# Cutting each head's loads into pieces and moving the projections away from the start of a half, in a Trainium2 attention kernel

## The reference, cut to what matters

```python
heads, dim_head = (16, 64)
x = layer_norm(x, ln_m_g, ln_m_b)          # the context, 6404 rows of 128
lat = layer_norm(latents, ln_l_g, ln_l_b)  # the tokens, 1024 rows of 128
q = lat @ Wq
kv_input = jnp.concatenate([x, lat], axis=1)   # 7428 keys
kv = kv_input @ Wkv
k, v = jnp.split(kv, 2, axis=-1)
dots = jnp.einsum('bhid,bhjd->bhij', q, k) * scale
attn = jax.nn.softmax(dots, axis=-1)
out = jnp.einsum('bhij,bhjd->bhid', attn, v)
return out @ Wout
```

## Time and profile before

| | |
|---|---|
| median of three runs | 2502.02 us |
| the profiled execution | 2494.57 us, span 2492.8 us |
| attention heads (first L608 to last L1000) | from 119.4 us to 2107.9 us |
| TensorE busy | 2303.6 us, 92% of the span |
| VectorE, ScalarE, GpSimd busy | 1864.0, 1673.9, 1846.9 us |
| moved by DMA | 165.57 MB |

### The profile page before, as it was taken

One profiled execution on the slowest core, in us unless ns is written; L12 is line 12 of the kernel. 1 busy time (PEld: TensorE's weight loads), 2 busy tenths in 40 slices (PEclk: granted clock), 3 DMA queues, 4 the chain that ended last, 5 costly groups with the idle time before them and its releaser, 6 DMA issues. The chain is left out here.

```text
span 2492.8 us, 68127 instructions
## 1 busy us (share of the span) xinstructions
PE 2303.6 (92%) x27961; PEld 1491.0 (60%) x27961; DVE 1864.0 (75%) x2822; ACT 1673.9 (67%) x3037; POOL 1846.9 (74%) x1105
## 2 busy tenths in 40 slices
PE   2999999999999999999999999999999998689987
PEld 1365665566566655665666556655666556558875
DVE  8877777887787878877877787878777761467754
ACT  4677777777677777776777677767777776246642
POOL 1798888989888988898889888888889998120000
PEclk9899999999999999999999999999999999889988
DMA  2612223132413141414131413141313000600000
GB/s 87 164 40 57 72 79 99 49 83 67 111 38 96 56 122 36 97 56 122 36 93 60 118 40 94 61 117 40 93 61 88 2 2 10 186 10 2 2 4 9
DMA packets 107639, 165.57 MB, mean 66 GB/s; under 512 B 23544, under 2 KB 97216, under 8 KB 102208
## 3 DMA queue, kind: packets, MB, share of 16 engines
q1 hardware_dynamic: 104032, 157.12, 23.0%
q10 hardware_dynamic: 3296, 4.10, 0.5%
HBM read 99.22 MB, written 61.97 MB: 65 GB/s over the span
## 5 line engine op out<-in xcount | busy, mean ns | idle before, releaser
L608 POOL TENSOR_TENSOR att_prob_low<-att_prob 128x1024 f16<-128x1024 f32 x960 | 1765.5, 1865 | 230.0 <-PE all_banks L728 126.4
L885 ACT ACTIVATE att_prob<-all_banks 128x512 f32<-128x512 f32 x1888 | 1070.7, 591 | 366.3 <-PE all_banks L693 247.7
L979 DVE TENSOR_REDUCE att_part<-all_banks 128x2 f32<-128x1024 f32 x800 | 946.5, 1218 | 197.9 <-PE all_banks L653 197.9
L714 PE MATMUL all_banks<-att_v,att_prob 128*128 128x129 f16 x5664 | 584.1, 221 | 2.8 <-DVE shared_att L1003 0.6
L714 PEld LDWEIGHTS all_banks<-att_v,att_prob 128*128 128x128 bf16 x5664 | 414.6, 98 | 238.0 <-issue 10.8
L728 PEld LDWEIGHTS all_banks<-att_v,att_prob_low 128*128 128x128 f16 x7552 | 328.8, 98 | 138.4 <-POOL att_prob_low L608 18.7
L674 PE MATMUL all_banks<-att_qc,att_kc 128*128 128x512 f16 x1056 | 401.3, 380 | 0.0
L675 PE MATMUL all_banks<-att_qd,att_kd 128*128 128x512 f16 x1056 | 401.0, 380 | 0.0
L728 PE MATMUL all_banks<-att_v,att_prob_low 128*128 128x65 f16 x7552 | 386.0, 194 | 13.4 <-POOL att_prob_low L608 13.4
L718 PE MATMUL all_banks<-att_v,att_prob 128*128 128x64 f16 x1888 | 371.2, 197 | 0.0
L716 PE MATMUL all_banks<-att_v,att_prob 128*128 128x65 f16 x1888 | 365.9, 194 | 0.0
(11 more groups left out here) (304 smaller groups left out, 3074.8 us busy)
## 6 DMA issues: line engine op xcount, KB each, us to landing
att_kc<-k_high SPq DMA_DIRECT2D x30, 928.5 KB, 10.8
att_v<-v_all SPq DMA_DIRECT2D x14, 1870.5 KB
v_all<-att_stage_v SPq DMA_DIRECT2D x98, 258.0 KB, 2.4
att_kd<-k_low SPq DMA_DIRECT2D x16, 928.5 KB, 15.0
k_high<-att_stage_h SPq DMA_DIRECT2D x98, 128.0 KB, 1.7
k_low<-att_stage_l SPq DMA_DIRECT2D x98, 128.0 KB, 1.9
att_kd<-k_low SPq DMA_DIRECT2D x16, 208.0 KB, 15.7
prep_ctx<-in_ctx SPq DMA_DIRECT2D x5, 640.0 KB, 9.1
```

What stands on the lines that cost most here:

```text
L608: pool.tensor_tensor(prob_low[g % NL][:, 0:w], p[:, 0:w], p.bitcast(BF16)[:, 1:2 * w:2], op=ALU.subtract).then_inc(low_split, 1)
L714: pe.matmul(O[:, q, :], w, v[:, e, t, :], start=first, stop=False, skip_group_check=True)
L885: act.activation(prob[g % NP][:, i * BANK:(i + 1) * BANK], S[n % 3], ACT.Exp, scale=SCALE)\
L979: dve.tensor_reduce(parts[:, n:n + 2], pers.banks[:, 4 + 2 * pair:6 + 2 * pair, :], axis=AX.X, op=ALU.max)\
```

## The change

The 7 transfers of `load_kq` become 16 and the 2 of `load_v` become 5: kc (twice) and the low part of K in four quarters each, and V in four parts and its tail. In each of periods 0 to 7 SyncE issues two pieces of K and Q. The pieces of V follow one per period, from period 8 in an even head and from period 24 in an odd one. From period 1 on SyncE first waits until the scores before that period are done, with a projection or without. The lists of periods are new: period 0 has no task in any head, and period 15 has none either. The counts in the waits on `k_in` and `v_in` follow.

```diff
-        KQ_AT = sorted([*range(0, PERIODS, 2), 9, 19])
-        V_AT = [w for w in range(23) if w % 3 != 2 and w != BACK_AT]
+        KQ_AT = [1, 3, 5, 7, 9, 11, 12, 14, 16, 17, 19, 20, 22, 23, 25, 26, 28]
+        V_AT = [1, 3, 4, 6, 7, 9, 10, 12, 14, 16, 17, 19, 20, 22, 23]
+        KQ_PIECES, V_PIECES, FIRST_K = 16, 5, 4
...
-            def load_kq(m):
+            def load_kq(m, x):
                 e = m % 2
-                sp.dma_start(kc[0:DH, e, 0:KEYS], k_high[rows(m), :]).then_inc(k_in[e], 16)
-                sp.dma_start(kc[DH:P, e, 0:KEYS], k_high[rows(m), :]).then_inc(k_in[e], 16)
-                sp.dma_start(qc[0:DH, e, :], q_high[rows(m), :]).then_inc(q_in[e], 16)
-                sp.dma_start(qc[DH:P, e, :], q_low[rows(m), :]).then_inc(q_in[e], 16)
-                sp.dma_start(qd[DH:P, e, :], q_high[rows(m), :]).then_inc(q_in[e], 16)
-                sp.dma_start(kd[DH:P, e, 0:KEYS], k_low[rows(m), :]).then_inc(k_in[e], 16)
-                load_upper(m)
+                c = slice(x % 4 * KEYS // 4 // 4 * 4, (x % 4 + 1) * KEYS // 4 // 4 * 4)
+                if x < 4:
+                    sp.dma_start(kc[0:DH, e, c], k_high[rows(m), c]).then_inc(k_in[e], 16)
+                elif x < 8:
+                    sp.dma_start(kc[DH:P, e, c], k_high[rows(m), c]).then_inc(k_in[e], 16)
...
+                elif x == 11:
+                    load_upper(m)
+                else:
+                    sp.dma_start(kd[DH:P, e, c], k_low[rows(m), c]).then_inc(k_in[e], 16)
...
-                    if w == 0 and b + 1 < HEADS:
-                        if b:
-                            sp.wait_ge(scored, b * HEAD_TILES)
-                        if b and e:
+                    if w == 0 and b and b + 1 < HEADS:
+                        sp.wait_ge(scored, b * HEAD_TILES)
+                        if e:
                             for r in range(NR):
                                 sp.wait_ge(kq_out[r], kq_writes(i + 2, r))
-                        if b == 0:
-                            sp.wait_ge(filled, 1)
-                        load_kq(b + 1)
-                        if b and not e:
+                    elif w == 0 and b == 0:
+                        sp.wait_ge(filled, 1)
+                    elif w:
+                        sp.wait_ge(scored, place(b, 2 * w))
+                    if 2 * w < KQ_PIECES and b + 1 < HEADS:
+                        load_kq(b + 1, 2 * w)
+                        load_kq(b + 1, 2 * w + 1)
+                    if KQ_PIECES // 2 <= w < KQ_PIECES // 2 + V_PIECES and b and not e:
+                        if w == KQ_PIECES // 2:
                             sp.wait_ge(low_done, LOW0 + b * UNITS)
-                            load_v(b + 1)
+                        load_v(b + 1, w - KQ_PIECES // 2)
```

More of the change, by code:

```diff
@@ L437, in next_period, with keys_in @@
             return (b, w + 1) if w + 1 < PERIODS else (b + 1, 0)
+        def keys_in(e, turn):
+            return 16 * (KQ_PIECES - 3) * (turn + 1 - (e == 0)) + (16 * FIRST_K if e == 0 else 0)
         def unit_of(n):
@@ L507, in load_v @@
[L507 to L512, removed]
+                c = slice(x % 4 * KEYS // 4 // 4 * 4, (x % 4 + 1) * KEYS // 4 // 4 * 4)
[3 more added lines that the diff above has]
+                    sp.dma_start(kc[DH:P, e, c], k_high[rows(m), c]).then_inc(k_in[e], 16)
+                elif x == 8:
+                    sp.dma_start(qc[0:DH, e, :], q_high[rows(m), :]).then_inc(q_in[e], 16)
+                elif x == 9:
+                    sp.dma_start(qd[DH:P, e, :], q_high[rows(m), :]).then_inc(q_in[e], 16)
+                elif x == 10:
+                    sp.dma_start(qc[DH:P, e, :], q_low[rows(m), :]).then_inc(q_in[e], 16)
+                elif x == 11:
+                    load_upper(m)
+                else:
+                    sp.dma_start(kd[DH:P, e, c], k_low[rows(m), c]).then_inc(k_in[e], 16)
@@ new lines, in load_v @@
+            def load_v(m, x):
+                e = m % 2
+                if x < V_PIECES - 1:
+                    t = [FULL_TILES * y // (V_PIECES - 1) for y in (x, x + 1)]
+                    sp.dma_start(v[:, e, t[0]:t[1], :].rearrange("p t c -> p (t c)"),
+                                 v_all[m * P:(m + 1) * P, t[0] * VCOLS:t[1] * VCOLS]).then_inc(v_in[e], 16)
+                else:
+                    sp.dma_start(v[0:TAIL, e, FULL_TILES, :],
+                                 v_all[m * P:m * P + TAIL, FULL_TILES * VCOLS:KEY_TILES * VCOLS]).then_inc(v_in[e], 16)
@@ L550, in _ @@
                             write_v(i + 1, n)
[L551 to L555, removed]
+                        if e and 0 < w - V_AT[-1] <= V_PIECES:
+                            if w == V_AT[-1] + 1:
+                                for r in range(NR):
+                                    sp.wait_ge(v_out[r], v_writes(i + 2, r))
+                                sp.wait_ge(low_done, LOW0 + b * UNITS)
+                            load_v(b + 1, w - V_AT[-1] - 1)
         @block.gpsimd
@@ L646, in window @@
                     pe.wait_ge(q_in[e], 48 * (turn + 1))
-                    pe.wait_ge(k_in[e], 64 * (turn + 1))
+                    pe.wait_ge(k_in[e], keys_in(e, turn))
                 for x in range(WINDOW):
@@ L698, in sums_free @@
                 if g == 0 and turn:
-                    pe.wait_ge(v_in[e], 32 * turn)
+                    pe.wait_ge(v_in[e], 16 * V_PIECES * turn)
                 elif g == 0:
@@ L830, in _ @@
             pe.wait_ge(q_in[0], 48)
-            pe.wait_ge(k_in[0], 64)
+            pe.wait_ge(k_in[0], keys_in(0, 0))
             score(0)
```

## The result

The changed kernel takes 2456.22 us (median of four runs, 2455.94 to 2456.86). The kernel before, run beside it, takes 2500.45 us. The ratio is 0.9827, with a 95% interval of 0.981 to 0.9844. The profiled execution of the changed kernel took 2455.94 us, with a span of 2454.1 us. Against the profiled execution of before that is 38.6 us less, where the medians differ by 44.2.

A forecast was written before the change was run, and what follows sets the result against it. The attention stage was taken as bound by two nearly full engines, GpSimd and TensorE. Gains of 5.2 + 10.8 + 19.6 = 35.6 us took the profiled 2494.57 to 2459.0; plus 7.4 to the median, 2466 us, range 2454 to 2486.

The forecast's parts named there:

- item 3: Periods 4 to 7 of even heads, 2 and 3 of odd: loads in pieces end waits for staging-buffer writes; 19.6 us.
- Item 1: Start of even heads: moving the task from period 0 to period 1 saves 0.74 us in seven heads, 5.2 us.
- item 2: Periods 0 and 15 of odd heads: moving their tasks elsewhere saves 0.77 us at 14 places, 10.8 us.
- Item 4: Other task moves, chiefly a new task in period 17 right behind one in 16: cost taken as 0, at most 10.4 us.
- first rival: Periods 16 and 17: VectorE is still behind there, so the penalty moves, costing up to 10.4 us; 2476 us, 10%.
- Item 5: Loads of each head: twelve more transfers and a SyncE wait per period cost 0.
- slow rival: Small transfers come one by one, TensorE stands 10.6 us at period 12 in each of 15 heads; 2625 us, 3%.
- second rival: Staging-buffer writes stay late because they share the queue with any load, leaving 16.0 us of gain; 2486 us, 7%.

The follow-up runs named there:

- pieces_only: The changed kernel with the two old task-period lists put back, loads still in pieces; 2469.53 us, ratio 0.9893.
- early_rest_late: pieces_only with the last addition of a half's normalization moved behind the next period's maxima and seed; 2447.12 us.
- three_kq_buffers: The kernel before with a third staging buffer for Q and K, V keeping two; 2478.99 us, ratio 0.9932.
- lists_only: The kernel before with only the two new task-period lists, loads left whole in one burst; 2457.05 us, ratio 0.9845.
- whole_123: lists_only with the even head's first three tasks in periods 1, 2, 3 in place of 1, 3, 5; 2505.84 us, ratio 1.0029.
- pieces_123: The changed kernel, loads in pieces, with the even head's first three tasks in periods 1, 2, 3; 2459.17 us, ratio 0.9833.
- whole_rest_late: lists_only with the last addition of a half's normalization moved behind the next period's maxima and seed; 2437.04 us.
- rest_late: The changed kernel with the last addition of a half's normalization moved behind the next period's maxima and seed; 2433.12 us, ratio 0.9746.

## Why the prediction was right, and where it was not

The direction and the mechanisms of the stalls were right, and the time lies in the range. The point, 2466 us, is 10 us too slow, and the range holds the time partly by luck. It names a spread of some 8 us, but its lower end, 2454, is 12 us down; with 8 us it would have begun at 2458, above the measured 2456.22. And the step that failed (item 3) did not show in the time, because the lists and the pieces remove the same stall.

*Item 1 and item 2, no task in period 0 or 15: right.* 9.55 us was taken from the second half of head 8, and 9.55 to 9.58 us is what all these stretches became. The two terms were 16.0 us together. Between the profiles of pieces_only and of the changed kernel heads 1 to 13 differ by 14.9 us, where the terms have 15.2 for these heads. early_rest_late shows the reason given, VectorE's queue in front of the maxima, and not only the place; the piece of the normalization that mattered there was its last addition, and its wait for GpSimd was not seen.

*Item 3, loads in pieces: the mechanism right, the attribution wrong, the size too small.* It is the late write of the staging buffer, as three_kq_buffers shows for the even heads with the burst left in place; for the odd heads no run takes the buffer away alone. The step that failed is that this gain was put down to the pieces. The lists move the third task of the even head from period 4 to 5, and of the odd head from 3 to 4, and the prediction never compared that with the landing of the write at 21.8 us, though the earlier trace rows has it. lists_only shows that the new lists alone let the copy come after the write, by 0.8 us: by the prediction's terms they were worth 16.0 us, and they gained 39.1. The pieces add nothing to the lists that can be measured; what they give is the margin, as whole_123 against pieces_123 shows, and four short waits of whole_rest_late. As to the size, heads 1 to 13 became 22.8 us shorter from before to pieces_only, where I had 19.6. Heads 4 to 12 lost 2.04 us each in periods 4 to 7 and not head 8's 1.84 (1.0 us over five heads), and odd heads lost also in periods 4 and 5: from 8.12 us, which I had taken for undisturbed, to 7.95 (with periods 2 and 3, which fell to 7.98, 2.2 us over seven heads).

*Item 4 and the first rival: nothing came back at the pair at 16 and 17.* Period 17 of the changed kernel takes 4.38 to 4.40 us with its task, 0.7 us above the 3.7 of a period with none, which is about the price of a task (0.59 to 0.65 us).

*Item 5, the pieces themselves: free, as costed.* lists_only and the changed kernel have the same head lengths (123.35 and 123.35, 122.89 and 122.92 us), with 12 more transfers in the one. The slow rival (transfers one by one, TensorE standing at period 12) is excluded by this. The second rival (the writes stay late) is excluded by pieces_only, whose tasks stand where they stood and whose list has no wait for a write. The Trainium skill's rule in "DMA: Bandwidth & Descriptors", section "Bandwidth", to batch DMAs to 1 MiB or more, did not decide here: 232 KB each cost nothing beside 928.5 KB, because their time is covered either way.

*The sum and its base.* 35.6 us were forecast and 38.6 are between the two profiled executions. 37.7 of them are in heads 1 to 13, where the terms have 34.8; the difference is item 3's 3.2 us, less 0.3 of items 1 and 2. The larger miss, 7.1 us, is the step from the profiled execution to the median. I added the whole 7.4 us by which before's median lay above its profile. But the changed kernel's median is 0.3 us above its own. Why that distance went is open. It may have belonged to the stalls: the changed kernel, pieces_only and rest_late, which have none, run within 0.9 to 1.6 us each, and the kernel before over 12 us, its mean clock at 0.970 to 0.980 against 0.979 in every run of the changed one. A fall of the clock at a stall is shown in whole_123, six times in six, and once in the profile of before, in the stretch of head 2 that the earlier trace rows has at 0.91. But before's other runs were timed without a trace, and their clock and time do not go strictly together (2496.14 us at 0.978, 2499.87 us at 0.978, 2491.85 us at 0.976). And lists_only, pieces_123 and early_rest_late spread over 3.8, 4.1 and 2.9 us without such a stall in their profiles, so a spread alone proves none. The time outside the heads varies as well: the profile of pieces_123 is 4.3 us longer than that of the changed kernel, though its heads 1 to 13 are no longer (1598.6 and 1599.0 us).

## What to carry to other kernels

Before a stall is put down to a transfer's size, write down when the late thing lands and when its consumer would ask for it, and look at what each edit does to both times. Two edits that each meet the same deadline do not add up. Work that nobody waits for belongs behind the work that another engine waits for, even where the engine is only three quarters busy; here one small addition moved behind the maxima gained half as much as the whole change. The distance from a profiled execution to the median is not a constant that a faster version keeps: here it was 7.4 us before and 0.3 us after.

## What the runs showed of the hardware

TensorE's granted clock fell to 0.50 for 6.8 us at each of the six stands of TensorE of 5.5 to 6.2 us in whole_123, beginning before TensorE worked again. Of the stands of 1.6 to 2.0 us in even heads of the kernel before, only the longest, 2.01 us, was followed by a spell, of 3.4 us; one of 2.18 us in three_kq_buffers was too.

The addition on VectorE (128x192, both inputs in SBUF) took 0.36 us with no instruction of GpSimd running, and otherwise ended 0.21 us after GpSimd's: 0.73 or 0.88 us in the kernel before, 0.38 us at nearly all its later places in rest_late, 2.00 us at one that began 0.10 us after a GpSimd instruction.
